# A pairwise-interaction tower on one core: sums over 8 products instead of 16, other DMA splits and another first-chunk order

## What is computed

```python
e = stack([tbl_f[ids[:, f]] for f in range(40)], axis=1)       # (2048, 40, 64)
p, q = e[:, rowidx], e[:, colidx]                              # all pairs i < j
z = einsum('bie,fie,bif->bi', p, param, q)                     # (2048, 780), param (64, 780, 64)
h = concatenate([z, dense_ctx], axis=1)                        # 796 columns
h = maximum(h @ W_top1 + b_top1, 0)                            # 512
h = maximum(h @ W_top2 + b_top2, 0)                            # 256
y = h @ W_top3                                                 # (2048, 1)
```

## Time and profile before

| | us |
|---|---|
| three executions | 1325.03, 1328.95, 1330.66 (median 1328.95) |
| the profiled execution | 1318.43 |
| its span in the profile | 1316.6 |
| PE busy | 1274.1 (97%) |
| DVE busy | 1014.7 (77%) |
| ACT busy | 1024.4 (78%) |
| POOL busy | 578.7 (44%) |

### The profile page before, as it was taken

One profiled execution on the slowest core, in us unless ns is written; L12 is line 12 of the kernel. 1 busy time (PEld: TensorE's weight loads), 2 busy tenths in 40 slices (PEclk: granted clock), 3 DMA queues, 4 the chain that ended last, 5 costly groups with the idle time before them and its releaser, 6 DMA issues.

```text
span 1316.6 us, 23698 instructions
## 1 busy us (share of the span) xinstructions
PE 1274.1 (97%) x6064; PEld 542.5 (41%) x6064; DVE 1014.7 (77%) x1680; ACT 1024.4 (78%) x7945; POOL 578.7 (44%) x615
## 2 busy tenths in 40 slices
PE   5689999999999999999999999999999999999999
PEld 2233444444444344443444444444344444444433
DVE  4388888888887787778887787788787777788870
ACT  0057987776568998999957998899968898899971
POOL 4455555555655555555345555555225553000000
PEclk9799999999999999999999999999999999999999
DMA  4512222222222222222112221222111222111100
GB/s 142 160 44 67 68 69 50 63 68 50 82 66 50 67 69 68 66 66 65 48 52 69 72 68 44 69 69 69 50 56 46 69 69 61 29 47 46 42 1 1
DMA packets 32896, 80.83 MB, mean 61 GB/s; under 512 B 11492, under 2 KB 12004, under 8 KB 32632
## 3 DMA queue, kind: packets, MB, share of 16 engines
q1 hardware_dynamic: 12128, 57.17, 13.7%
q0 software_dynamic: 19456, 19.96, 7.4%
q10 hardware_dynamic: 1176, 2.19, 0.5%
HBM read 79.27 MB, written 0.01 MB: 60 GB/s over the span
## 4 chain that ended last, share of the span: by engine, by line
PE 80%; ACT 10%; DMA 3%; DVE 3%; issue 2%; POOL 2%; ACTq 0%; DVEq 0%
PE ring L689 35%; PE z_ps L712 18%; PE ring L694 16%; ACT wide_prod L503 9%; PE ring L718 7%; PE ring L663 3%; DMA rows<-tbl,idx_now 2%; POOL rows L443 2%; PE ring L722 2%; DVE wide_prod L581 1%; DVE prod L568 1%; ACT e_t L464 1%; PE ring L725 0%; DVE z_b L592 0%; PE ring L670 0%
## 5 line engine op out<-in xcount | busy, mean ns | idle before, releaser
L503 ACT ACTIVATE wide_prod<-wide_prod 128x64 f32<-128x64 f32 x3904 | 933.5, 242 | 46.6 <-DVE wide_prod L581 22.8
L443 POOL DMA_INDIRECT rows<-tbl,idx_now x608 | 577.9, 950 | 524.2 <-DMA rows<-tbl,idx_now 302.2
L568 DVE TENSOR_TENSOR prod<-ring,e_t 128x512 f32<-128x512 f32 x1008 | 627.8, 682 | 172.7 <-PE ring L689 119.9
L503 ACT ACTIVATION_READ_ACCUMULATOR wide_prod<-wide_prod 128x1 f32 x3904 | 737.4, 189 | 21.1 <-issue 20.1
L689 PE MATMUL ring<-e_t,w 64*128 64x512 f32 x2176 | 607.7, 616 | 8.7 <-ACT e_t L464 6.4
L581 DVE TENSOR_TENSOR wide_prod<-ring,rows 128x512 f32<-128x512 f32 x512 | 327.6, 682 | 70.2 <-PE ring L694 56.8
L689 PEld LDWEIGHTS ring<-e_t,w 64*128 64x128 f32 x2176 | 255.0, 187 | 281.7 <-issue 176.0
L694 PE MATMUL ring<-w,e_t 64*128 64x512 f32 x1024 | 317.5, 615 | 2.7 <-DVE wide_prod L581 1.4
L712 PE MATMUL z_ps<-prod,strip 128*32 128x512 f32 x2096 | 253.1, 595 | 0.9 <-DVE prod L568 0.7
L694 PEld LDWEIGHTS ring<-w,e_t 64*128 64x128 f32 x1024 | 119.1, 187 | 134.4 <-issue 79.1
L712 PEld LDWEIGHTS z_ps<-prod,strip 128*32 128x32 f32 x2096 | 65.3, 109 | 179.9 <-issue 150.7
(11 more groups left out here) (23 smaller groups left out, 80.0 us busy)
## 6 DMA issues: line engine op xcount, KB each, us to landing
w<-weights SPq DMA_DIRECT2D x64, 768.0 KB
rows<-tbl,idx_now POOLq DMA_INDIRECT x608
w<-weights SPq DMA_DIRECT2D x4, 512.0 KB
z_t<-tbl SPq DMA_DIRECT2D x8, 250.0 KB
w<-w1z SPq DMA_DIRECT2D x1, 1792.0 KB, 18.3
h<-hot_ids ACTq DMA_DIRECT2D x6, 250.0 KB
w<-w2p SPq DMA_DIRECT2D x1, 512.0 KB, 12.3
z_t<-hot_ids ACTq DMA_DIRECT2D x2, 250.0 KB
```

Source lines behind the costliest of these rows:

```text
L443: nc.gpsimd.indirect_dma_start(out=rows[:, slot, t, E * f:E * f + E], out_offset=None, in_=tables[m * 2 + f], in_offset=bass.IndirectOffse ...
L503: last = nc.scalar.activation(products, products, ACT.Copy, accum_out=z_b[:, h, t, col:col + 1])
L568: nc.vector.tensor_tensor(dst[:, j, :], ring[:, bank, :], e_t[:, k, :], ALU.mult).then_inc(t_free, 1)
```

## The change

1. **Groups.** A group has 8 blocks (`SUMS`), so a chunk has 33 instead of 16; the last has 6. `Z_FIRST`, `GROUP_LAG`, `TILE_AT` and `STEP_AT` get new numbers.
2. **Loads of the head.** Each whole table is loaded as 112 and 13 partitions instead of 125 at once; the row numbers are broadcast to 128 partitions instead of 125. The five loads of the tower's weights stand behind piece 6 (`MLP_BEHIND`) instead of piece 2.
3. **First chunk.** The tiles are made in the order 4, 5, 6, 7, 0, 1, 2, 3, and the 8 units among tiles 4 to 7 stand ahead of all other items. The slots, groups and columns of weights follow this order (`UNIT_ORDER`, `BLOCK_ORDER`). SP's wait for tile 0 is thereby one for the fifth tile. PE's waits for `e_ready` are worked out anew (`TILE_WAITS`).

```diff
-GROUPS = NBLK // 16
-LONG_GROUPS = NBLK % 16
 COLS = 4
-GROUP_FIRST = [16 * g + min(g, LONG_GROUPS) for g in range(GROUPS + 1)]
-Z_FIRST = [0, 3, 6, 9, 12, 16]
+SUMS = 2 * COLS
+GROUPS = -(-NBLK // SUMS)
+GROUP_FIRST = [min(SUMS * g, NBLK) for g in range(GROUPS + 1)]
+Z_FIRST = [0, 7, 13, 19, 25, GROUPS]
...
-HOT_P, HOT_J = 125, 8
-HOT_AT = {0: (4, 5), 1: (6,), 3: (7,)}
-FIRST_TILES = [4, 0, 5, 1, 6, 2, 7, 3]
+HOT_P, HOT_J, HOT_SPLIT = 125, 8, 112
+HOT_AT = {0: (4, 5, 6), 2: (7,)}
+FIRST_TILES = [4, 5, 6, 7, 0, 1, 2, 3]
...
-TILE_AT = [-23, -14, -14, -1, -1, 8, 8, 10, 20, 20, 26, 37, 53, 66, 78, 83, 103, 116, 140, 165]
-STEP_AT = [34, 50, 89, 103, 126, 140, 153]
+TILE_AT = [-23, -14, -14, -1, -1, 8, 8, 8, 20, 20, 29, 37, 56, 66, 75, 75, 112, 112, 150, 171]
+STEP_AT = [33, 50, 90, 103, 126, 137, 165]
...
-GROUP_LAG = [4, 2, 4, 6, 5, 4, 4, 5, 4, 4, 6, 6, 4, 4, 4, 3]
+GROUP_LAG = [8, 7, 6, 5, 7, 5, 3, 6, 5, 5, 5, 6, 6, 6, 5, 5, 4, 4, 4, 5, 4, 5, 4, 5, 4, 5, 5, 5, 4, 4, 4, 3, 5]
...
-    items = units[:head]
+    hot = [item for item in units if UNITS[item[1]][0] in ONE_HOT]
+    items = hot + units[:head]
     for m in range(FIXED, TILES):
-        row = [item for item in units if UNITS[item[1]][0] == m]
+        row = [item for item in units if UNITS[item[1]][0] == m and item not in hot]
...
+MLP_BEHIND = 2 * W_SLOTS
...
+def unit_place(c, u):
+    first = [v for v in range(NU) if UNITS[v][0] in ONE_HOT] if c == 0 else []
+    return first.index(u) if u in first else u + sum(v > u for v in first)
+
+UNIT_ORDER = [sorted(range(NU), key=lambda u: unit_place(c, u)) for c in range(CHUNKS)]
+UNIT_PLACE = [[UNIT_ORDER[c].index(u) for u in range(NU)] for c in range(CHUNKS)]
+BLOCK_ORDER = [[b for u in UNIT_ORDER[c] for b in BLOCKS_OF[u]] for c in range(CHUNKS)]
...
             def load_tables(i):
                 for h in range(2):
-                    pos = 2 * ONE_HOT[i] + h
-                    sp.dma_start(hot_table[2 * i + h], tables[pos].rearrange("(p j) e -> p (j e)", j=HOT_J)
-                                 ).then_inc(hot_in[i], 16)
+                    table = tables[2 * ONE_HOT[i] + h].rearrange("(p j) e -> p (j e)", j=HOT_J)
+                    for part in (slice(0, HOT_SPLIT), slice(HOT_SPLIT, HOT_P)):
+                        sp.dma_start(z_t[part, 2 * i + h, :], table[part, :]).then_inc(hot_in[i], 16)
...
             for piece in range(1, W_SLOTS):
                 load(piece)
-            for dst, src in ((b1[:, :], b1c), (b2[:, :], b2c), (w3[:, :], w3c), (w2[:, :, :], w2p), (w1[:, :], w1z)):
-                sp.dma_start(dst, src).then_inc(mlp_in, 16)
             for piece in range(W_SLOTS, len(PIECES)):
                 sp.wait_ge(t_ready, through(PIECES[piece - W_SLOTS][2]))
                 load(piece)
+                if piece == MLP_BEHIND:
+                    for dst, src in ((b1[:, :], b1c), (b2[:, :], b2c), (w3[:, :], w3c), (w2[:, :, :], w2p),
+                                     (w1[:, :], w1z)):
+                        sp.dma_start(dst, src).then_inc(mlp_in, 16)
...
-                    act.dma_start(hot_idx[q], hot_ids[q:q + 1, :].broadcast_to([HOT_P, NB])).then_inc(hot_in[i], 16)
+                    act.dma_start(hot_idx[q], hot_ids[q:q + 1, :].broadcast_to([P, NB])).then_inc(hot_in[i], 16)
...
-                if FIRST_OF[c, m] == n:
-                    pe.wait_ge(e_ready, max(T_NUMBER[c * TILES + k] for k in range(m + 1)) + 1)
+                if n in TILE_WAITS:
+                    pe.wait_ge(e_ready, TILE_WAITS[n])
```

More of the change, by code:

```diff
@@ L201, in prep_at @@
     if c == 0:
-        if m in ONE_HOT:
-            m -= ONE_HOT[0]
-        first = FIRST_OF[0, max(m, 1)]
-        return first if m < ONE_HOT[0] else first - m
+        first = FIRST_OF[0, 5 if m == 4 else max(m, 1)]
+        return first if m <= ONE_HOT[-1] else first - m
     return c * NI + TILE_AT[m]
@@ L216, in last_of_group, with groups_with @@
     c, g = divmod(group, GROUPS)
-    return PLACE[c, "unit", BLOCKS[GROUP_FIRST[g + 1] - 1][0]]
-def groups_with(c, u):
-    return c * GROUPS + group_of(BLOCKS_OF[u][-1]) + 1
+    return PLACE[c, "unit", BLOCKS[BLOCK_ORDER[c][GROUP_FIRST[g + 1] - 1]][0]]
+def groups_with(c, place):
+    return c * GROUPS + group_of(BLOCK_ORDER[c].index(BLOCKS_OF[UNIT_ORDER[c][place]][-1])) + 1
 def turn_at(half):
@@ L302, with tiles_of, tile_waits @@
 BANKS, BEFORE = bank_plan()
+def tiles_of(item):
+    c, kind, i = item
+    if kind == "wide":
+        return [*range(FIXED), WIDES[i][0]]
+    m, k = UNITS[i]
+    return [m, k] if k < m else [m, m - 1]
+def tile_waits():
+    waits, most = {}, 0
+    for n, item in enumerate(ITEMS):
+        need = max(T_NUMBER[item[0] * TILES + m] for m in tiles_of(item)) + 1
+        if need > most:
+            waits[n] = most = need
+    return waits
+TILE_WAITS = tile_waits()
 def bilinear_tower(nc, tables, idx, hot_ids, dense_t, weights, w1z, b1c, w2p, b2c, w3c, out):
@@ L339, in bilinear_tower @@
         hot_table = [z_t[0:HOT_P, q, :] for q in range(len(SMALL))]
-        hot_idx = [(h1[0:HOT_P, q, :] if q < KH1 else h2[0:HOT_P, q - KH1, :] if q < KH1 + KH2
-                    else z_t[0:HOT_P, q + len(SMALL) - KH1 - KH2, :]).bitcast(I32) for q in range(len(SMALL))]
+        hot_idx = [(h1[:, q, :] if q < KH1 else h2[:, q - KH1, :] if q < KH1 + KH2
+                    else z_t[:, q + len(SMALL) - KH1 - KH2, :]).bitcast(I32) for q in range(len(SMALL))]
         hot = [wide_prod[0:HOT_P, q // 2, q % 2, :] for q in range(2 * WIDE_SLOTS)]
@@ L555, in unit @@
                 m, k = UNITS[u]
-                number = c * NU + u
+                number = c * NU + UNIT_PLACE[c][u]
                 if number >= PROD_SLOTS:
@@ L597, in one_hot @@
                 i = ONE_HOT.index(tile)
-                dve.wait_ge(hot_in[i], 4 * 16)
+                dve.wait_ge(hot_in[i], 6 * 16)
                 for j in range(HOT_J):
@@ L608, in one_hot @@
                                 dve.wait_ge(hot_used, before + 1 - before // (2 * HOT_J))
-                        nc.vector.tensor_scalar(hot[number % len(hot)], hot_idx[2 * i + h], first_row_f[0:HOT_P, :],
+                        nc.vector.tensor_scalar(hot[number % len(hot)], hot_idx[2 * i + h][0:HOT_P, :], first_row_f[0:HOT_P, :],
                                                 float(j), ALU.subtract, ALU.is_equal).then_inc(hot_ready, 1)
@@ L646, in look_up_tile @@
                 dst = take_bank(("tile", tile))
-                pe.wait_ge(hot_in[i], 4 * 16)
+                pe.wait_ge(hot_in[i], 6 * 16)
                 for j in range(HOT_J):
@@ L707, in sum_group @@
                 first, end = GROUP_FIRST[Z_FIRST[t]], GROUP_FIRST[Z_FIRST[t + 1]]
-                for b in range(GROUP_FIRST[g], GROUP_FIRST[g + 1]):
+                for i in range(GROUP_FIRST[g], GROUP_FIRST[g + 1]):
+                    b = BLOCK_ORDER[c][i]
                     u, jj = BLOCKS[b]
-                    v = b - first
-                    col, r = v % COLS, v // COLS
+                    col, r = (b - first) % COLS, (b - first) // COLS
                     last = nc.tensor.matmul(z_ps[32 * col:32 * col + 32, :], strip[:, 30 - 2 * r:62 - 2 * r],
-                                            prod[:, (c * NU + u) % PROD_SLOTS, jj, :], start=r == 0,
-                                            stop=b + COLS >= end)
+                                            prod[:, (c * NU + UNIT_PLACE[c][u]) % PROD_SLOTS, jj, :],
+                                            start=i < first + COLS, stop=i + COLS >= end)
                 last.then_inc(summed, 1)
```

## The result

| | before | changed |
|---|---|---|
| median of the executions (us) | 1327.51 (4: 1325.03 to 1330.66) | 1277.02 (4: 1271.84 to 1279.70) |
| the profiled execution | 1318.43 | 1274.63 |
| its span | 1316.6 | 1272.8 |

The ratio is 0.9614, with a 95% interval of 0.9572 to 0.9656: 50 us faster, where 78 had been forecast.

What follows compares the result with a forecast made beforehand. PE was taken as bound, losing 22 of 307 us a chunk as long sums stop DVE for slots. Head 69 + chunk 0 304 + periods 587 + rest 278 = 1238 us span, 1250.5 from the median; range 1222 to 1294.

Steps and rivals of the forecast that it cites:

- rival A: Chunks: ACT takes over as the bound, 305 us a period, chunk 0 gives 20, head 7, so 1296 us; chance 0.16.
- A sign of being wrong: Chunks: periods over 300 us with PE waiting for e_t or z_t copies would show the forecast wrong.
- Rival B: Whole kernel: everything hides, 287 us a period, head 65, chunk 0 292, so 1224 us; chance 0.10.
- slots that a group frees too late: Long sums on PE: DVE runs out of slots and stops 2.68 us until the burst ends; small groups remove this.
- a burst of 2 us is covered by a ring: Sums on PE: the ring holds 7 x 0.60 = 4.2 us of DVE's work, enough for the shorter burst.
- rival D: Chunks: PE waits for ACT's copy of z_ps, 25 us a period, so slower, 1346 or 1356 us; chance 0.05.
- Chunk 0's term: From the first wide to chunk 0's first tower step: 304 us instead of 335.9, so -32 (-44 to -18).
- I take 286.5 + 7 = 293.5 us a chunk: Period: PE's work of 286.5 us plus 7 of the 22 lost, for ACT's late tiles or banks; bounds 287 to 305.
- ACT asks for 283 to 292, and the slots tide over most of what differs between places: Period: ACT's own need is 283 to 292 us a chunk, with local differences mostly covered by slots.
- It can be 17, the 4 slots x 4.3: Chunk's end: ACT, today about 8 us behind, may lag 17 us, the 4 slots of wide_prod x 4.3.
- now a group stands in it too: 69, so -7 us: Head: tile 3 at 62, then 4.9 us and a group, first wide at 69 us, so -7 (-13 to +2).
- stay close: Chunk 0: the gathers remain near their limit, sharing 22 us of further waits; two halves of 6.4 us and more a tile.

Runs made afterwards that it cites:

- the run with pairs: Changed kernel with its groups of 8 summed two at a time, four items behind the last unit of the second: 1348.02 us, ratio 1.0178.
- 10 slots: Changed kernel with 10 instead of 12 units' slots in prod (PROD_SLOTS), nothing else: 1262.51 us, ratio 0.9590.
- the early groups: Changed kernel with chunk 0's first two groups summed ahead of items 9 and 11 instead of 12 and 15: 1260.55 us, ratio 0.9600.
- tiles unspread: Without the change to the changed kernel that prepares the next chunk's tiles 1, 2, 3 at 18, 13, 7 items before its start (1268.24 us with it).
- no more sums on DVE: Without moving further reductions from ACT to DVE in the changed kernel; with 16 a chunk moved it took 1274.58 us, with 8 a chunk 1270.58.
- the three together: Changed kernel with chunk 0's first two groups earlier, the next chunk's tiles spread, and 8 reductions a chunk on DVE: 1268.53 us, ratio 0.9632.

## Why the prediction was right and wrong

**The number.** The median of 1277.0 lies in the stated range of 1222 to 1294, but outside the 1232 to 1268 that the forecast claimed for itself, and nearer to rival A's 1296 than to the 1250.5. A sign of being wrong that it named came true: periods over 300 us, with PE waiting for copies to e_t. The span exceeds the forecast by 34.8 us and the median by 26.5. The 8 us between come from carrying the sum from spans to medians with the 10.5 us of the kernel before, where the changed kernel's own distance was 2.4; that is luck. Rival B's 1224 does not follow from its terms: 4 us in the head, 12 in chunk 0 and 6.5 in each of three chunks below 1250.5 are 1215. And A's own 1296 lies outside the range that was to hold most of A.

**What bounded the kernel** was read half rightly. That PE's long bursts stop DVE, and PE with it, is shown: the groups alone give 0.9629. (The new tables that go with them were not run apart, but the run with pairs has most of them too and loses the gain.) The reason given, slots that a group frees too late, was read from one stretch and holds for 6 of 32 groups. At the others DVE had used up the ring during the burst. The run with pairs has hardly a stop for slots and no gain, and with 10 slots the gain stays. So the shorter burst, which the text had as its second reason ("a burst of 2 us is covered by a ring"), is the likelier cause; no run with more slots and groups of 16 separates the two fully.

The changeover is 0.26 us a group, and no wait of PE names a copy of z_ps (rival D). Chunk 0's term, 304, was measured as 303.5, if in part by luck: with the early groups it was 308.9, 5.8 of them at item 220.

**The step that failed** is "I take 286.5 + 7 = 293.5 us a chunk: of the 22 us lost, 7 stay". 17.5 and 15 stayed; with the last stretch that is 26.6 us more than the forecast had. The text named a place for this loss, tiles and banks for which ACT is late, and priced it too low. It said "ACT asks for 283 to 292, and the slots tide over most of what differs between places"; the trace shows ACT behind by its reductions just where tiles must be copied, each such copy holding a bank of a ring that is given back in order, and 0.5 to 3 us of PE go there at a time. "It can be 17, the 4 slots x 4.3" was the other half of this: a lag was counted as cover, but a lag is also what the copies wait behind. That is not the whole of it. The named waits for copies are 5.9 us of the 32.5 lost in the two periods, and with 10 slots, where they are 0.5 us, 20.9 are still lost, 10.5 a chunk and not 7. The forecast had no term for DVE's pace at a full ring, which is seen in the changed kernel's trace; how much of the rest is DVE's, and how much a sum of PE's work that is too low, stays open. Rival A (305 a period, 1296 in all) was closer in the periods than the forecast, where ACT pauses for 27 us; on chips 6 and 14, with tiles unspread and no more sums on DVE, the periods of 295 to 299 are 2 to 5 us above the forecast's. Its sum failed in chunk 0, where it gave 20 us and 32 came, and in the head, as the forecast's did.

**The head**, "now a group stands in it too: 69, so -7 us", was measured as +1.3. The loads did what they should: PE begins at 10.72 us (8 forecast, 16.17 before). By the Trainium skill (DMA: Bandwidth & Descriptors, Rules for kernel authors) transfers under 64 KB pay mostly overhead. The prediction's working of that rule, 8 such parts one after another for 16 us more, is what the trace disagrees with: the start moved 5.5 us forward with the 8 parts of 26 KB in the queue. What one such part costs no run shows. But tile 3 came at 65.67 (62 forecast, range to 72): the gather under pieces 1 and 2 waited 5.45 us, once more than counted. And two groups, not one, stood behind that wait, the first at half the clock: 69.47 to 73.05 against 75.87 to 77.72 for the same 16 records. Putting them ahead of it brought the first wide to 70.16, so this account is shown. Run again, the changed kernel had its first wide at 75.34 (tile 3 at 63.12), so the head itself varies by 2 to 3 us.

**What the prediction did not see** is the floor of the gathers. It put them into "stay close" with a share of 22 us in chunk 0, and read their pace in the earlier trace rows; it did not multiply it by 22 tiles. They did not hold the changed kernel in its own trace, but they can take back what a better head wins: with early groups and with the three together PE stood there for 5.77 and 8.95 us, and even with 10 slots and the old head for 5.79. Whether loads and order add anything to the groups stays open. On chip 15 they do not (0.9649 against 0.9629 on chip 14), where the lead was gone within one period; on chip 6 the changed kernel with 10 slots has 0.9590. Both parts were never run against the groups alone on one chip.

## What to carry to other kernels

A burst on the busiest engine must be shorter than what the ring between the engines holds, with the lead that is left at the worst place and not the full one; cutting it in two was worth 3.7% here, and joining two again made the changed kernel 5.5% slower (1348.02 against 1277.53). When a bound is removed, sum up each other engine's pace from its start to the first place where it is needed (here 22 tiles x 13.4 us on POOL), besides its busy share. A lag of an engine with two kinds of work is not cover for the urgent kind: whoever queues behind it waits for all of it.
